# The second edge stage of a two-layer graph network: linear-attention products moved ahead of a turn's sums, and eight block numbers read at once on ScalarE

## The reference, cut to what matters

```python
# graph attention of layer 1, per edge e = (src, dst), 4 heads of 64
score = leaky_relu(a_src[src] + a_dst[dst], 0.2)
w     = exp(score - segment_max(score, dst))
gnn   = segment_sum(w * h[src], dst) / segment_sum(w, dst) + bias
# linear attention of layer 1, per node, 8 heads of 32
q, k  = elu(q) + 1, elu(k) + 1
kv    = einsum('bnhd,bnhm->bhdm', k, v)
z     = 1 / (einsum('bnhd,bhd->bnh', q, k.sum(1)) + 1e-6)
mix   = einsum('bnhd,bhdm,bnh->bnhm', q, kv, z) @ w_out + b_out
x     = x + gnn + (mix and its norm)
```

## Time and profile before

| | |
|---|---|
| median of 3 runs | 2669.74 us (2667.49 to 2671.74) |
| the profiled execution, span from first to last instruction | 3152.6 us |
| span of the profiled execution less the median | 482.9 us |
| busy of the span | PE 59%, DVE 62%, POOL 54%, PEld 42%, ACT 32% |
| the second edge stage in the span | 2036 to 2890 us |

### The profile page before, as it was taken

The page is one execution under the profiler, slowest core; times in us unless marked ns, Lnnn a source line. Parts: engine busy times, 40 slices in busy tenths (PEclk is TensorE's granted clock), DMA queues, the critical chain, the costliest instruction groups (busy, mean ns, idle before and its releaser), DMA issues. The chain is left out here.

```text
span 3152.6 us, 49567 instructions
## 1 busy us (share of the span) xinstructions
PE 1869.4 (59%) x11708; PEld 1332.9 (42%) x11709; DVE 1956.5 (62%) x6206; ACT 1003.7 (32%) x2697; POOL 1696.0 (54%) x1693
## 2 busy tenths in 40 slices
PE   0045555756666666655888628556666666652499
PEld 0023232634444444442777515344444444441377
DVE  8686666467777777774333247566666666677534
ACT  0012221224444444434222215323333333332431
POOL 4777777446666666515665654265655655560200
PEclk9987776867777777856999959755555555555699
DMA  7000000053333333214323321232222222532401
GB/s 203 2 8 10 10 10 12 1 183 88 86 88 88 86 88 88 72 64 147 83 83 79 103 78 29 58 82 78 79 78 79 79 76 78 112 94 55 151 9 33
DMA packets 169043, 231.02 MB, mean 73 GB/s; under 512 B 72072, under 2 KB 127060, under 8 KB 168819
## 3 DMA queue, kind: packets, MB, share of 16 engines
q0 software_dynamic: 69328, 139.28, 16.5%
q1 hardware_dynamic: 99616, 90.61, 10.1%
HBM read 190.39 MB, written 39.38 MB: 73 GB/s over the span
## 5 line engine op out<-in xcount | busy, mean ns | idle before, releaser
L2365 POOL DMA_INDIRECT e_rows<-mid_table,rec x488 | 502.0, 1029 | 384.9 <-PE e_ps_A L2711 140.2
L986 POOL DMA_INDIRECT e_rows<-mid_table,e_rec x440 | 432.9, 984 | 273.5 <-issue 107.1
L256 POOL DMA_INDIRECT mid_sorted<-p_record,p_row x391 | 411.3, 1052 | 201.8 <-issue 116.0
L1172 PE MATMUL e_ps_A<-e_rows,e_hot 128*125 128x260 f32 x880 | 327.7, 508 | 1.5 <-DVE e_rows L1028 1.5
L256 POOL DMA_INDIRECT mid_sorted<-keep_record,keep_row x231 | 227.4, 984 | 183.3 <-PE x_ps_h L1692 79.9
L2711 PE MATMUL e_ps_A<-e_rows,room 128*32 128x65 f32 x3904 | 189.8, 310 | 178.4 <-issue 175.4
L2711 PEld LDWEIGHTS e_ps_A<-e_rows,room 128*32 128x32 f32 x3904 | 134.9, 162 | 230.3 <-issue 227.4
L2631 ACT ACTIVATE room<-room 128x66 f32 x488 | 125.2, 257 | 321.3 <-issue 209.0
L1157 PE MATMUL e_ps_T<-e_identb,e_hot 128*125 128x128 bf16 x440 | 87.0, 291 | 214.2 <-DVE e_hot L1009 108.6
L1172 PEld LDWEIGHTS e_ps_A<-e_rows,e_hot 128*125 128x125 f32 x880 | 197.9, 250 | 29.3 <-DVE e_rows L1028 2.4
L1662 DVE TENSOR_SCALAR x_hT<-x_ps_h,keep_b1T 128x128 f32<-128x128 f32 x256 | 72.1, 344 | 207.0 <-PE x_ps_y L1701 188.9
(11 more groups left out here) (615 smaller groups left out, 4507.5 us busy)
## 6 DMA issues: line engine op xcount, KB each, us to landing
mid_expert_in<-p_zrow SPq DMA_DIRECT2D x1, 8192.0 KB
w<-in_L_ffn_w SPq DMA_DIRECT2D x16, 512.0 KB
x_w<-in_L_ffn_w SPq DMA_DIRECT2D x16, 512.0 KB
x_y<-in_L_ffn_b SPq DMA_DIRECT2D x64, 128.0 KB
x_xs<-mid_expert_in SPq DMA_DIRECT2D x64, 128.0 KB
mid_expert_out<-x_y SPq DMA_DIRECT2D x64, 128.0 KB
f_w_all<-in_L_ffn_W SPq DMA_DIRECT2D x16, 512.0 KB
e_rows<-mid_table,rec POOLq DMA_INDIRECT x488
```

Source lines behind the costliest of these rows:

```text
L256: pool.indirect_dma_start(out=to, out_offset=bass.IndirectOffsetOnAxis(ap=row[:, t:t + 1].bitcast(U32), axis=0), in_=record[:, t, :], in_o ...
L986: pool.indirect_dma_start(out=rows[:, s % RING * 2 + j, :], out_offset=None, in_=k["table"], in_offset=bass.IndirectOffsetOnAxis(ap=rec[:, ...
L1172: last = nc.tensor.matmul(ps_A[0:NP, q % 4, 0:ROW], hot[:, q * 2 + j, :], rows[:, q * 2 + j, :], start=j == 0, stop=j == 1)
L2365: pool.indirect_dma_start(out=rows[:, j, q, :], out_offset=None, in_=k["table1"], in_offset=bass.IndirectOffsetOnAxis(ap=rec[:, i * TG + q ...
```

## The change

- The results of `numerators` and `outputs` move from `ps_mT` to the free part of the bank of `ps_S`.
- On PE they are issued ahead of `turn_hot` and the sums. `numerators(t)` now comes in tile t's even turn, the turning in the next even turn (ahead of `turn_marked`), `outputs` in the odd turn after that. PE waits for the scores to have been read (`s_sc`) ahead of both, and for DVE to have used them (`divided`, `added`) ahead of `spread_to_edges`.
- DVE divides in even turns and adds the outputs of tile t-2 in odd ones, in the same place at the turn's end; `s_top` is gone.
- ACT keeps the turned rows in the next even turn, stages q in odd turns, squares in even ones, and reads the eight block numbers of a turn ahead of its first copy, without the check of each.

```diff
--- before.py
+++ after.py
@@ -2238,11 +2238,13 @@
         ps_hT1 = m.banks("ps_hT", 1)
         ps_hT = ps_hT1[:, 0, :].bitcast(BF16).rearrange("p (t e) -> p t e", t=TG)
         ps_mT = m.banks("ps_mT", 2)
-        ps_S = m.ps("ps_S", [P, 2 * TG, SPLIT * H])
+        ps_S1 = m.banks("ps_S", 1)
+        SPREADS = 2 * TG * SPLIT * H
+        ps_S = ps_S1[:, 0, 0:SPREADS].rearrange("p (x a) -> p x a", x=2 * TG)
         ps_A2 = m.banks("ps_A", 4)
 
-        ps_num = ps_mT[0:NP, 0, 0:DC * (P + 4)].rearrange("p (c n) -> p c n", c=DC)
-        ps_out = ps_mT[0:NP, 1, 0:D]
+        ps_num = ps_S1[0:NP, 0, SPREADS:SPREADS + DC * (P + 4)].rearrange("p (c n) -> p c n", c=DC)
+        ps_out = ps_S1[0:NP, 0, SPREADS:SPREADS + D]
         ps_attT = ps_hT1[:, 0, 0:DC * NP].rearrange("p (c n) -> p c n", c=DC)
 
         s_in = m.sem("nodes_in")
@@ -2274,7 +2276,6 @@
         s_done = m.sem("averaged")
         s_out = m.sem("written")
         s_q = m.sem("q_staged")
-        s_top = m.sem("marked_scores_read")
         s_num = m.sem("mix_numerators")
         s_den = m.sem("mix_denominators")
         s_rz = m.sem("mix_reciprocals")
@@ -2437,8 +2438,7 @@
                 o.settle()
                 o.done(v.tensor_tensor(most[:], most[:], tiles_of(owns, i), ALU.max))
                 add(1)
-                o.settle_alone()
-                dve.sem_inc(s_top, 1)
+                o.settle()
                 o.done(v.tensor_tensor_scan(tiles_of(tops, i, 1), tiles_of(same, i), most[:], column(tops, i * TG), ALU.mult, ALU.max))
                 add(2)
                 o.settle()
@@ -2539,12 +2539,12 @@
                 o.done(v.tensor_tensor(xs, xs, spread(gbias.unsqueeze(1), NP, TB, D), ALU.add))
 
             def odd(t):
+                if a_tile(t - 2):
+                    add_mix(t - 2)
+
+            def even(t):
                 if a_tile(t):
                     divide(t)
-
-            def even(t):
-                if a_tile(t):
-                    add_mix(t)
 
             def step(i, j, u):
                 over = u is None
@@ -2623,9 +2623,11 @@
 
             def keep_sums(i, j):
 
+                _, blocks = nc.values_load_multi_w_load_instructions(
+                    k["bin1"][0:1, bass.ds(i * TG, TG)], engines=[mybir.EngineType.Activation], min_val=0, max_val=G1_BINS - 1,
+                    skip_runtime_bounds_check_because="each is a count of blocks begun, less one")
                 wait_alone(act, s_acc, i * TG + TG)
-                for q in range(TG):
-                    block_of = act.value_load(k["bin1"][0:1, bass.ds(i * TG + q, 1)], min_val=0, max_val=G1_BINS - 1)
+                for q, block_of in enumerate(blocks):
                     if not (known(i) and i == 0 and q == 0):
                         wait_alone(act, s_keep, i * TG + q)
                     nc.scalar.activation(acc[:, bass.ds(block_of, 1), :].rearrange("p a w -> p (a w)"), state[:, j, q, :],
@@ -2642,25 +2644,31 @@
                 nc.scalar.activation(q, k["qT"][:, bass.ds(t, 1), :, :].rearrange("p a c n -> p (a c) n"), ACT.Copy).then_inc(s_q, 1)
 
             def keep_attT(t):
-                if a_tile(t):
-                    wait_alone(act, s_attT, t + 1)
-                    nc.scalar.activation(attT, ps_attT, ACT.Copy).then_inc(s_attTk, 1)
+                wait_alone(act, s_attT, t + 1)
+                nc.scalar.activation(attT, ps_attT, ACT.Copy).then_inc(s_attTk, 1)
 
             def add_squares(t):
                 wait_alone(act, s_h, t + 1)
                 nc.scalar.activation(square, row_of(normed, t), ACT.Square, accum_out=k["ms"][:, bass.ds(t, 1)]).then_inc(s_sq, 1)
 
+            def turned_mix(t):
+                if a_tile(t):
+                    keep_attT(t)
+
             def odd(t):
-                if a_tile(t - 1):
-                    add_squares(t - 1)
+                if a_tile(t):
+                    stage_q(t)
 
             def even(t):
-                if a_tile(t + 1):
-                    stage_q(t + 1)
+                if a_tile(t - 2):
+                    add_squares(t - 2)
+
+            def nothing(t):
+                pass
 
             def step(i, j, u):
                 if u is not None:
-                    mixing(i, j, u, lambda t: None, keep_attT)
+                    mixing(i, j, u, nothing, lambda t: turned_mix(t - 1))
                 if not (known(i) and (i < 1 or i > TURNS)):
                     act.wait_ge(s_sc, i)
                     nc.scalar.activation(ex[:], score[:], ACT.Exp).then_inc(s_ex, 1)
@@ -2722,24 +2730,21 @@
 
             def step(i, j, u):
                 if u is not None:
+                    mixing(i, j, u, nothing, lambda t: turn_mix(t - 1, i))
                     turn_marked(i)
-                    mixing(i, j, u, lambda t: None, room_for_hot)
+                    mixing(i, j, u, lambda t: outputs(t - 2, i), lambda t: numerators(t, i))
+                    mixing(i, j, u, nothing, lambda t: turned_mix_kept(t - 1))
                     turn_hot(i + 1, (j + 1) % RING)
                 if not (known(i) and i < 1):
                     add_up(i - 1, (j - 1) % RING)
                 if u is not None:
-                    mixing(i, j, u, lambda t: numerators(t, i), lambda t: outputs(t, i))
+                    mixing(i, j, u, lambda t: added(t - 2), divided)
                     spread_to_edges(i, j)
-                    mixing(i, j, u, lambda t: turn_mix(t, i), lambda t: None)
-
-            def room_for_hot(t):
-                if a_tile(t):
-                    wait_alone(pe, s_attTk, t + 1)
 
             def numerators(t, i):
                 if a_tile(t):
-                    wait_alone(pe, s_top, i + 1)
                     wait_alone(pe, s_q, t + 1)
+                    wait_alone(pe, s_sc, i)
                     for c in range(DC):
                         last = mm(ps_num[:, c, :], q[:, c, :], kvz[:, c, :], start=True, stop=True)
                     last.then_inc(s_num, 1)
@@ -2747,18 +2752,33 @@
             def turn_mix(t, i):
                 if a_tile(t):
                     wait_alone(pe, s_att, t + 1)
-                    wait_alone(pe, s_hTk, i + 2)
+                    wait_alone(pe, s_hTk, i + 1)
                     for c in range(DC):
                         last = nc.tensor.transpose(ps_attT[:, c, :], att[:, c * P:(c + 1) * P], k["ident"][0:NP, 0:NP])
                     last.then_inc(s_attT, 1)
 
             def outputs(t, i):
                 if a_tile(t):
-                    wait_alone(pe, s_top, i + 1)
+                    wait_alone(pe, s_attTk, t + 1)
+                    wait_alone(pe, s_sc, i)
                     for c in range(DC):
                         mm(ps_out, attT[:, c, :], wout[:, c, :], start=c == 0, stop=False)
                     mm(ps_out, k["one"][0:1, 0:NP], bout[0:1, :], start=False, stop=True).then_inc(s_mix, 1)
 
+            def turned_mix_kept(t):
+                if a_tile(t):
+                    wait_alone(pe, s_attTk, t + 1)
+
+            def divided(t):
+                if a_tile(t):
+                    wait_alone(pe, s_att, t + 1)
+
+            def added(t):
+                if a_tile(t):
+                    wait_alone(pe, s_h, t + 1)
+
+            def nothing(t):
+                pass
 
             pe.wait_ge(s_const, 1)
             mm(ps_mT[:, 0, 0:G1_N], k["one"][0:1, :], bins[:], start=True, stop=True).then_inc(s_bin, 1)
```

## The result

| | before | after |
|---|---|---|
| median | 2669.74 us (2667.06 to 2671.74, 7 runs) | 2661.30 us (2657.85 to 2663.87, 7 runs) |
| ratio | | 0.997 (95% interval 0.996 to 0.998) |

The kernel became 8.4 us faster, 0.3%; 50 us were predicted. The time lies inside the predicted range, in the part that the rival "POOL becomes the bound" had given (2656 to 2666 us).

A forecast was written before the change was run, and what follows sets the result against it. The prediction took the chain through PE's products and DVE's use of them as the bound; 48 us from the turns plus 4 from block numbers, less handoffs, gave about 50 us off, 2620 us, range 2590 to 2668.

The forecast's parts named there:

- POOL becomes the bound: Second edge stage: eight gathers take 10.1 to 10.7 us a turn, so the gain is 0 to 10 us plus 4; chance 0.25.
- Then DVE sets the turn: Mixed turns after the change: DVE's work makes 18.6 us a pair against 20.5, 48 us over 25 pairs; chance 0.52.
- the assumption of the first part: Second edge stage: PE's stops without a releaser, 134.1 us in 174, are part of the recording and absent from timed executions.
- the stops: PE's waits at the sums for no releaser the profile shows, 134.1 us in 174 within 50 turns of the recorded execution.
- The arithmetic of the chains: Mixed turns without the stops: a pair takes about 20.5 us before and 18.6 us after, from summed engine work.
- the 48 us of the term: Mixed turns: products ahead of the sums bring a pair from 20.5 to 18.6 us, 1.9 x 25 = 48 us.
- the rival with real stops: PE's sums: 5.9 us each gains 107 us (chance 0.05), 8.9 loses 43 (0.08 with late handoffs); break-even 8.05.
- The turning's wait: PE's turning waits for ACT's emptying of the one-hot bank; moving it to the next even turn saves 0.5 us a pair.
- The handoff: New wait ahead of `spread_to_edges`: 0.5 to 0.6 us under DVE's 1.22 us mark, costing nothing; 0 to 0.3 us allowed.
- The block numbers: ACT's copies at the stage's end come 0.45 us apart instead of 0.65, gaining 4 us, bounds 0 and 9.
- The rival of a slow reading: ACT: eight readings at 0.73 us take 5.8 us, ACT sets the turn, 52 us lost, 2722 us; chance 0.03.
- its last sentence but one: Sign in the changed profile: if DVE's mark waits for `e_rows`, POOL is the bound.

The follow-up runs named there:

- experiments 4 and 5: Unchanged and changed kernel, each with six of a turn's eight gathers from turn 4 on: 2641.37 us (0.9890 of before) and 2604.33 us (0.9758).
- experiments 8 to 12: Against before under the longer condition: DVE's mark halved (0.9851, 0.9847), DVE's scores ahead of the mark (0.9942, 0.9955), both on the changed kernel; changed kernel itself 0.9814.
- experiment 1: The unchanged kernel recorded once more, no edit: 2668.88 us, span 2667.1 us.
- experiment 10: The changed kernel itself, run again under the longer condition: 3058.62 us against 3116.73 of before, 0.9814.
- experiment 2: Unchanged kernel with only the eight block numbers read at once, products left behind the sums: 2663.49 us against 2668.51, 0.9979.
- experiment 5: The changed kernel with six of a turn's eight gathers from turn 4 on: 2604.33 us, 0.9758 of before.

## Why the prediction was wrong

**The step that failed** is "Then DVE sets the turn", and behind it the assumption of the first part, that the stops belong to the recording. In its place POOL sets the turn, before and after. The arithmetic of the chains was right: 20.5 and 18.6 us a pair were forecast, and 20.5 and 19.0 came out once POOL was relieved (experiments 4 and 5). But they were forecast for kernels in which nothing else takes 9.3 us a turn, and eight gathers take 10.1 by the prediction's own sum. Before stood at 10.38 us and after at 10.34. Of the 48 us of the term, 25 pairs of 1.5 us, 37, are there to be had once POOL is faster, and 37.0 were measured; 3.4 were paid out, and not by the waits that the prediction removed but by gathers that DVE holds up for less.

**How the rival was underrated.** It was worked out and named with its sign to look for (the mark waits for `e_rows`), and it gave 2656 to 2666 us; its chance of 0.25 was too low for what the rows in hand said. The argument against it was that 482.9 us were hard to place in a stage in which POOL can't be faster. It needed no faster gather: between the two conditions their mean went only from 1029 to 999 ns, and their idle time from 384.9 to 211.5 us. Of the 485.5 us between the two spans this stage holds 195 (817.8 us from its first to its last mark against 622.6), in turns that POOL sets in one trace and PE's stops in the other; other stages hold the rest. The argument with weight was the one for it: the row of a gather and its pause, times eight, is a floor of the turn whatever the stops are.

**The stops** are no product of recording. Kernels that show them in the profile take as long in their other executions (experiments 8 to 12), and in each of the ten traces of the shorter condition none of the 3,904 records of the sums has a stop of over 0.1 us ahead of it. What the rival with real stops said, a gain of 107 us or a loss of 43 with the length of the sum deciding, held in its mechanism, since the sum grew; at its mean of 8.2 us the rival's formula gives a pair of 27.6, and 25.3 was measured, so, if PE sets the turn there, the fixed part of its chain was 2.3 us too long, which keeps the kernel on the gaining side: 25 pairs of 2.5 us are 62, and 58 were measured. What makes the stops stays open: before had them in one set and not in another on the same chip. They are not PE's alone: ACT's copies (L2631) stood still 209.0 us in 189 stops without a releaser in the recorded before, and 7.3 us in 15 in experiment 1. The granted clock of TensorE does not decide them either: in experiment 10 they precede 121 of the 1,279 records of the sums that ran at 2.4 GHz and 290 of the 2,625 at 1.2, about as often.

**The turning's wait** for the one-hot bank exists (43.8 us in 24 turns in experiment 1) and was hidden, as everything else of PE and ACT is under POOL's 10.38 us.

**The handoff** of the scores cost nothing, as forecast, though it is longer than its 0.5 to 0.6 us: PE starts the scores 0.36 us behind DVE's use of the product (forecast 0.1), and DVE could start 0.39 later, 0.75 together, under the mark's 1.22.

**The block numbers** were forecast at 4 us with bounds 0 and 9, and gave 5.0 (experiment 2). The copies come 0.38 to 0.43 us apart (forecast 0.45), and the reading for which 2.2 us were put down takes 0.55. The rival of a slow reading failed with it.

**The sum** of what was measured is 3.4 + 5.0 = 8.4 us. What the prediction wanted seen was right for the waits at L2531 and L2520, for outputs ahead of the one-hot (2005.29 against 2008.28), for the copies under 0.5 us apart and for the end of the stage; and its last sentence but one, on `e_rows`, names what happened.

## What to carry to other kernels

Before a chain is shortened, multiply out every engine's own work per turn, gathers with their pause included, and set it beside the turn to be reached: a chain that is the longest in a disturbed trace may lie under such a floor. When span and timed median differ by 18%, take a second trace before reading the first, since the waits it shows may belong to neither kernel. When POOL sets the turn, what DVE does during a gather counts: its wide two-operand instructions are best started just behind the start of a gather, and fewer waits on DVE are no gain by themselves.

## What the runs showed of the hardware that was not expected

- **A gather held by DVE ends at a fixed time.** One of 128 rows takes 0.95 us and 0.30 to the next, with 1,056 bytes a row as with 32. If it starts while a DVE instruction of 1.22 us with two operands in SBUF runs, it ends 2.05 us behind that instruction's start, however far into it it began: started 0.05 us in it took 2.00, at 0.12 1.93, at 0.35 1.69 (experiment 5), at 0.46 1.59 and at 0.88 1.17. Started less than 0.04 us in, it took its 0.95. Behind a half-size mark of 0.69 us the end came 1.52 us behind its start. Both are 0.83 us behind the end of DVE's instruction; over the ten traces of the shorter condition all 632 gathers held by marks and weights end 0.82 to 0.84 us behind it.
- **One reading of eight register values** on ACT takes 0.55 us, one of a single value 0.27.
- **The same two kernels stand at 0.997 or at 0.981** of each other, by the condition under which they run.
